# Unread whole-array matmuls ahead of each projection stage, up to six per attention step

## The reference, cut to what matters

```
q = x@Wq (16 heads of 64), kv = x@Wkv (128 wide), k = kv@Wk (32 per head), v = kv@Wv (32 per head)
q = rms_norm(q)[..., :32], k = rms_norm(k)
p = softmax(causal(q@k.T / 8));  a = (p@v padded to 64 per head) @ Wo
x = layernorm(x + a)
# bit-linear feed-forward: activations rounded to int8 per row, weights to -1, 0, 1 by their mean |w|
h = silu(bit(x, w_gate)) * bit(x, w_up)          # inner width 4096
y = layernorm(x + bit(h, w_down))
```

## Time and profile before

| | |
|---|---|
| median of 3 runs | 1576.91 us |
| the profiled execution | 1579.0 us, span of the slowest core (4) 1577.5 us |
| spans of the eight cores | 1565.3 to 1577.5 us |
| PE busy | 1312.7 us, 83% |
| ACT busy | 828.2 us, 53% |
| DVE busy | 805.3 us, 51% |
| steps before the feed-forward begins | from about 92 to about 560 us of the span |

### The profile page before, as it was taken

How to read it: one execution, slowest core, us unless ns; L and a number is a source line. 1 busy time by engine, 2 the same in 40 slices (tenths; PEclk the granted TensorE clock), 3 DMA queues, 4 the chain that set the end, 5 groups by cost and what they waited for, 6 DMA issues and landing times.

```text
span 1577.5 us, 22882 instructions; the slowest of 8 cores (1565.3 to 1577.5 us)
## 1 busy us (share of the span) xinstructions
PE 1312.7 (83%) x7494; PEld 441.5 (28%) x7494; DVE 805.3 (51%) x1158; ACT 828.2 (53%) x998; POOL 327.6 (21%) x350
## 2 busy tenths in 40 slices
PE   2667578789976787879988998989985999999997
PEld 0212122222211122222322222222232444444443
DVE  2327864666555656642664234323364767273743
ACT  2576466687976765757766786847810121020200
POOL 1025421244210203050203212050113002020320
PEclk9966566755866589989999999989998999999999
DMA  9996795768545377663353633162336868586783
GB/s 251 305 282 182 228 260 160 195 206 267 187 154 187 99 245 221 216 134 107 128 147 117 157 105 91 60 161 61 130 125 183 270 201 220 187 202 227 178 222 119
DMA packets 146513, 283.06 MB, mean 179 GB/s; under 512 B 91744, under 2 KB 92000, under 8 KB 133088
## 3 DMA queue, kind: packets, MB, share of 16 engines
q1 hardware_dynamic: 144816, 272.70, 56.9%
q0 software_dynamic: 1584, 8.91, 3.5%
HBM read 235.96 MB, written 33.55 MB: 171 GB/s over the span
## 4 chain that ended last, share of the span: by engine, by line
PE 60%; DVE 11%; DMA 10%; issue 8%; ACT 8%; POOL 1%; SPq 1%; DVEq 0%; ACTq 0%; POOLq 0%
PE ps_w L1001 13%; PE ps_sc L1001 8%; PE ps_sc L830 7%; PE ps_w L1124 6%; ACT PT L843 5%; DMA R<-wffn 5%; PE ps_sc L1124 4%; PE ps_den L785 4%; PE ps_w L547 3%; PE ps_pv L796 3%; PE ps_w L716 2%; DVE qb L382 2%; PE ps_pv L1001 2%; PE ps_den L1001 2%; DMA khat<-wq 2%
## 5 line engine op out<-in xcount | busy, mean ns | idle before, releaser
L843 ACT ACTIVATE PT<-ps_sc,negM 128x1024 bf16<-128x1024 f32 (+3 forms) x640 | 593.7, 984 | 202.4 <-PE ps_sc L830 199.3
L1001 PE MATMUL ps_w<-R,S 128*128 128x512 fp8e4 x1032 | 272.1, 389 | 22.4 <-DVE xsC L957 6.7
L830 PE MATMUL ps_sc<-qn,khat 32*128 32x512 bf16 (+3 forms) x1280 | 210.9, 403 | 61.4 <-ACT PT L843 57.3
L851 POOL TENSOR_TENSOR PT<-PT,tri 128x512 bf16<-128x512 bf16 x64 | 80.7, 1262 | 418.7 <-ACT PT L843 417.2
L785 PE MATMUL ps_den<-PT,ones 128*32 128x512 bf16 (+3 forms) x1280 | 132.9, 405 | 8.1 <-DVE S L774 7.1
L1124 PE MATMUL ps_w<-R 128*128 128x512 fp8e4 x448 | 121.8, 402 | 20.9 <-DMA R<-R 18.4
L856 POOL TENSOR_SCALAR PT<-PT,hflag_sb 128x512 bf16<-128x512 bf16 x64 | 119.7, 1870 | 75.3 <-ACT PT L843 74.3
L796 PE MATMUL ps_pv<-PT,vtok 128*32 128x512 bf16 (+3 forms) x1280 | 130.6, 399 | 0.0
L1001 PEld LDWEIGHTS ps_w<-R,S 128*128 128x128 bf16 x1032 | 83.6, 99 | 164.8 <-issue 97.5
L830 PEld LDWEIGHTS ps_sc<-qn,khat 32*128 32x128 bf16 x1280 | 54.0, 93 | 262.3 <-issue 257.5
L1014 ACT ACTIVATE R<-ps_w,xsT 128x512 f32<-128x512 f32 x76 | 52.3, 688 | 131.9 <-PE ps_w L1001 121.0
(11 more groups left out here) (199 smaller groups left out, 1507.8 us busy)
## 6 DMA issues: line engine op xcount, KB each, us to landing
R<-wffn SPq DMA_DIRECT2D x65, 1024.0 KB, 7.0
R<-scr_w SPq DMA_DIRECT2D x128, 512.0 KB, 4.5
wb<-scr_w SPq DMA_DIRECT2D x64, 512.0 KB, 5.1
scr_w<-qb SPq DMA_DIRECT2D x48, 256.0 KB, 6.1
khat<-wffn SPq DMA_DIRECT2D x11, 1024.0 KB, 12.2
vtok<-wffn SPq DMA_DIRECT2D x11, 1024.0 KB, 8.2
R<-xt POOLq DMA_DIRECT2D x7, 1024.0 KB, 14.7
R<-scr_x SPq DMA_DIRECT2D x12, 512.0 KB, 5.8
```

The source lines that it names most:

```text
L830: t = pe(lambda e, j=j, gi=gi, tc=tc, kc=kc, stc=stc: e.matmul(ps_sc[:, j * 512 + stc:j * 512 + 512], khat[32 * j:32 * j + 32, kc:kc + 128 ...
L843: t = act(lambda e, hf=hf, pp=pp, stc=stc: e.activation(PTr[pp][:, 2 * hf:2 * hf + 2, stc:512], PSr[:, 2 * hf:2 * hf + 2, stc:512], AF.Exp ...
L851: t = pool(lambda e, pp=pp, stc=stc: e.tensor_tensor(PTr[pp][:, :, stc:stc + 128], PTr[pp][:, :, stc:stc + 128], tri.rearrange("p (r n) -> ...
L1001: t = pe(lambda e, c=c, b=b, kw=kk[w], i=i: e.matmul(wring.bufs[b], xqT[u % 2][:, i * 1024 + c * 128:i * 1024 + c * 128 + 128], wbuf[kw][: ...
```

## The change: what it does, and the diff

A new function, `idle_mms(n)`, takes a bank of `ps_w` from the ring, issues n whole matmuls of 512 columns into it (weights `bd32`, moving data the first 512 columns of `qn`) and gives the bank back. Each of them waits for the release of that bank that its last user left; nobody reads what they write. While the projections are not done, the loop issues, ahead of a step's stages, as many as the step before fell short of six: six less the PE instructions that the stages of that step issued. In the three steps between the end of the projections and the start of the feed-forward it issues four per step.

```
+        def idle_mms(n):
+            w = wring.take()
+            for _ in range(n):
+                pe(lambda e: e.matmul(wring.bufs[w], bd32[:], qn[:, 0:512], start=True,
+                                      stop=True), [wring.free[w]])
+            wring.give(w, wring.free[w])
...
+        fill_mms = 0
         for part in attention():
             if not st["proj"]:
                 stages += 1.5 if t_tile[1] is None else 1.0
+                if fill_mms:
+                    idle_mms(fill_mms)
+                fill_mms = 6
                 while stages >= 1.0:
                     stages -= 1.0
+                    m = len(P.q["tensor"])
                     next(proj_it, None)
+                    fill_mms -= min(fill_mms, len(P.q["tensor"]) - m)
+            elif not ffn_on[0]:
+                idle_mms(4)
```

## The result

The changed kernel takes 1617.31 us (median; 1601.82 to 1618.11), the one before 1581.2 on the same chip. The ratio is 1.0205, with a 95% interval of 1.0155 to 1.0256: **slower**, and clear of noise, though whether by more than 2% is open. I had forecast 1565, and the range ended at 1596. A repeat on another chip gave 1.0211 [1.0178, 1.0244].

What follows compares the result with a forecast made beforehand. No engine is full; PE ends `queries2` steps at the low clock, ACT ends `keys_values2` steps. Terms -36 - 10 + 14 + 20 = -12 us, applied to the median 1576.9, gave 1565 us; range 1538 to 1596.

Steps and rivals of the forecast that it cites:

- slower, by fills at the low clock: Rival: fills at 1.2 GHz make steps 4.91 us; 1617 us with half the phase low, 1595 just past break-even; 18%.
- a gain of -32 at the top clock: Attention to feed-forward start: the first three terms' sum, in us, were the clock at the top throughout.
- Step 1: `queries2` and `latent2` steps, 59 groups of four matmuls: faster at the higher clock, -36 us.
- Step 2: Output projection, 16 groups alone on PE between DVE's additions: 0.85 us each at the higher clock, -10 us.
- Step 3: The 72 `keys_values2` steps: short ones stretch to 2.74 us, +14 us.
- Step 4: Whole phase: the clock falls after PE's waits, with 14% of the time low and fills then on the path, +20 us.
- clock under 0.85: Sign that the low-share term is wrong, with steps of 4.9 us and L818 back to back in the timeline.
- Step 5: New waits of fills for a bank's last reader: 0 to +3 us after L716, left at 0.
- The mark of this step: Sign that the new-waits term is wrong: L818 shows waits for DVE of more than 8 us in all.

Runs made afterwards that it cites:

- e8: The changed kernel with ScalarE's sums of absolute values taken over 64 columns instead of 2048; ratio 0.9997 to the kernel before the change.
- e9: The changed kernel with only fills (added matmuls) in groups of three or more, 337 of 423; ratio 1.0068 to the kernel before the change.
- e10: The changed kernel with only fills (added matmuls) in groups of one or two, 86 of 423; ratio 1.0075 to the kernel before the change.
- e2: The changed kernel with the same 423 fills on 32 of the array's 128 rows; 1738.6 us, ratio 1.0958 to the kernel before the change.
- e1: The changed kernel with each fill in the free bank given back longest ago, ring's turn unmoved; 1603.13 us, ratio 1.009 to the kernel before.

## Why the prediction was wrong

What came true is the rival "slower, by fills at the low clock". That its point value, 1617 with half of the phase low, is the measured time is chance: the low share was smaller (26%, and 36% on core 2), and by the rival's formula 26% makes -32 + 437 x 0.26 x 0.33 = +5.5 us, where the phase grew by 26.5. The rest is a gain of -32 at the top clock that was not there, and two waits priced at nothing. By the steps of the sum (means of the eight cores):

**Step 1, -36 forecast, +8.7 measured: the step that failed most.** I spread the low share of 73% evenly over all steps. The Q steps of tile 1 held 2.4 GHz for 41% of their time, tile 2's K/V steps for 10%, by the table above; I had read 0.99 in 402 to 420 and used it for the mechanism only. Only 16.5 Q steps per core went from low to the top, where I took 35. They went from 3.36 to 2.86 us, 0.50 each and not 1.1: -8.3 in all. PE did not end all of them: step 33 took 3.90 us at a share of 0.01 and 3.89 at 1.00, and 2.23 in e8, where ScalarE's sum is short. How much of the missing 0.6 us is ScalarE's and how much VectorE's no run separates. The 16.1 Q steps that were at the top already went from 2.17 to 2.45: +4.4 (with two fills and PE at the end of the step it is more, as in steps 88 to 90: 2.53, 2.05 and 2.44 became 2.95, 2.48 and 2.82), where I took 2. Those that went from mixed to the top gave -1.2. The rest, +13.8, are Q steps that are not at the top after, the two bank waits (7.9) among them.

**Step 2, -10 forecast, -2.5 measured,** of both tiles' projection steps: they were at 2.4 GHz for 0.48 of their time in tile 1 already, and in tile 2 they reach 0.55 only.

**Step 3, +14 forecast.** Where the clock is up, K/V steps cost only +1.9 in 49.2 steps. The 2.78 us seen is the 2.74 worked out, but the short steps had less of it to lose. This term was too large.

**Step 4, +20 at a low share of 14%.** The steps of 4.9 us are there (4.85), so the price per step was right. The share was not: 26% as a mean over the phase, 36% on core 2, which sets the time; and the mark "clock under 0.85" is met there (0.82 over the phase), though not by the mean of the cores (0.87). By the rival's own formula the change breaks even at 22%. I had taken the low share to go with PE's waiting per microsecond, against the feed-forward's stretch with its 10%. That rule failed, not the choice of rows: PE waited for DVE and DMA 63.3 us in all before, not 37.5, but 44.0 us in the other stretch, not 25.1, which makes a ratio of 1.7 for my 1.8. I had left out the waits on ACT: 21.1 us in 36 of up to 2.2 over the phase after, against 22.9 in 46 of at most 0.8 from 600 to 1160 of that trace. Per microsecond these are equal; only their length differs. That the length makes the difference is argued, no run isolates it, and what sets the share stays open. K/V steps in all are +22, of them +20 in steps that are not at the top after.

**Step 5, priced 0.** Its cover was "a reader that the next stage would wait for in the same step". That is false where a stage goes on in the bank that it holds: there it waits for nobody. Two steps, 7.9 us, shown by e9 and e10. The two steps behind the second, 84 and 85, took 3.49 and 3.36 us for 2.28 and 2.49; on core 2 nearly all of both is at 1.2 GHz (4.85 us each). The mark of this step, L818 waiting for DVE for more than 8 us, is met by far (36.8 us on core 2), but most of that L569 and others waited before: PE's waits on DVE did not grow in total (58.8 us before, 59.3 after), they moved to where they cost.

**What held.** That the clock would answer to whole matmuls and not to packed ones: e2 is the test, for those on 32 rows. The Trainium skill ("TensorE: Matmul & The Clock Gate", Part 1) has the clock follow how busy TensorE has been; with the profile's busy share in that place, e2's 0.92 busy at a clock of 0.55 disagrees more clearly than the row of the prediction did, since the change has the same instructions at the same places, with 0.81 busy at a clock of 0.82. The packed and whole costs of a step at each level, and the unchanged end, held too.

**What stays open:** what sets the low share of a stretch with fills; why it is highest on cores 2 and 6 in the change's trace, while no core stands out in e1's; and the mechanism behind the 6 us in tile 1's Q steps that neither e9 nor e10 has.

## What to carry to other kernels

Before raising a clock, ask which engine ends the steps in which it is low: a fast clock there buys nothing, and an unread matmul costs its full time in each step that PE ends (0.4 us for two at 2.4 GHz in the steps 88 to 90, 0.42 for one at 1.2, by 422.90 to 423.73 above). Count a filling instruction's buffer as a real one, with the last reader of the bank it takes, most of all where the work behind it would wait for nothing. If it is done at all, a few fills in the thin steps among or ahead of dense ones bring the gain (17 gave -0.4% and 80 -0.6%, not told apart; 423 gave +2.05%).

## What the runs showed that I had not expected

The clock is a result of the schedule as much as a cause: shortening ScalarE's sums, which touches no matmul, raised tile 1's share at 2.4 GHz from 0.40 to 0.53, and the kernel took 2.1% less time. And thin matmuls can hold it down: 423 of them on 32 rows took the share over the phase from 0.29 to 0.11.
